# State space stage of a two-layer decoder: the closing normalisation of each batch on ScalarE instead of VectorE, and a new order of the passage to the second mixer

## The reference, cut to what matters

```python
x = _layernorm(x + _L1_attn_ref(x, L1_attn_W_in, ...), axis=-1)

def _layernorm(x, axis=-1, eps=1e-05):
    m = jnp.mean(x, axis=axis, keepdims=True)
    v = jnp.var(x, axis=axis, keepdims=True)
    return (x - m) / jnp.sqrt(v + eps)

# _L1_attn_ref(u, ...), 8 heads of 64, state 128
z, xBC, dt = jnp.split(u @ W_in, ...)
xBC = silu(conv of 4 taps over xBC)
x, B, C = jnp.split(xBC, ...)
y = ssd(x * dt, A * dt, B, C, chunk)  # per head: (C B^T * decay) (x dt)
y = (y + x * D) * silu(z)
var = jnp.mean(jnp.square(y), axis=-1, keepdims=True)
y = y * jax.lax.rsqrt(var + EPS) * norm_scale
return y @ W_out
```

## Time and profile before

| | us |
|---|---|
| runs before, median of 3 (lowest, highest) | 782.22 (782.18, 782.72) |
| the profiled execution's own time | 784.08 |
| its span in the trace | 782.3 |
| PE busy | 722.9 (92%) |
| DVE busy | 626.2 (80%) |
| POOL busy | 538.8 (69%) |
| ACT busy | 409.6 (52%) |

### The profile page before, as it was taken

How to read it: one execution, slowest core, us unless ns; L and a number is a source line. 1 busy time by engine, 2 the same in 40 slices (tenths; PEclk the granted TensorE clock), 3 DMA queues, 4 the chain that set the end, 5 groups by cost and what they waited for, 6 DMA issues and landing times. The chain is left out here.

```text
span 782.3 us, 13429 instructions
## 1 busy us (share of the span) xinstructions
PE 722.9 (92%) x4286; PEld 499.0 (64%) x4286; DVE 626.2 (80%) x1279; ACT 409.6 (52%) x656; POOL 538.8 (69%) x782
## 2 busy tenths in 40 slices
PE   6999999999997899999869999989899999999994
PEld 5777777654442577777547777765544447767783
DVE  3878877789798777774949999987899999887774
ACT  0656666610415444443667778880000338788885
POOL 2767888877773543331156777789877988999962
PEclk9999999999998799999979999999999999999998
DMA  8900000000400400000031112203000000000001
GB/s 282 372 11 2 2 2 2 2 1 0 162 0 24 182 1 2 1 1 1 24 114 43 62 60 67 69 1 124 0 1 1 0 2 0 9 15 14 21 20 37
DMA packets 12867, 33.89 MB, mean 43 GB/s; under 512 B 2688, under 2 KB 8064, under 8 KB 11520
## 3 DMA queue, kind: packets, MB, share of 16 engines
...
## 5 line engine op out<-in xcount | busy, mean ns | idle before, releaser
L1126 PE MATMUL bank<-XT,win_late 128*128 128x256 f32 x320 | 87.8, 402 | 4.4 <-DVE ss_xc L1376 4.2
L684 DVE TENSOR_REDUCE MIX<-m_pr 128x128 f32<-128x1024 f32 x64 | 77.4, 1210 | 0.7
L632 POOL TENSOR_TENSOR m_kv<-CTXT 128x512 f32<-128x512 f32 x64 | 65.0, 1039 | 10.4 <-PE bank L657 10.3
L632 POOL TENSOR_TENSOR m_kv<-XT,CTXT 128x512 f32<-128x512 f32 x64 | 67.7, 1081 | 5.8 <-PE bank L657 5.8
L1376 DVE SCALAR_TENSOR_TENSOR ss_xc<-bank,cw_late,ss_xc 128x254 f32<-128x254 f32 x144 | 66.5, 477 | 4.0 <-ACT ss_xc L1249 0.5
L1126 PEld LDWEIGHTS bank<-XT,win_late 128*128 128x128 f32 x320 | 56.9, 195 | 19.3 <-DVE ss_xc L1376 12.2
L655 PE MATMUL bank<-m_kv,toep 128*128 128x512 f32 x128 | 67.0, 605 | 0.2
L656 PE MATMUL bank<-m_kv,toep 128*128 128x512 f32 x128 | 66.2, 599 | 0.0
L657 PE MATMUL bank<-m_kv,toep 128*128 128x512 f32 x128 | 65.7, 595 | 0.0
L541 POOL TENSOR_TENSOR f_ve<-f_mv,eps 128x1 f32<-128x1 f32 x48 | 9.5, 199 | 80.4 <-DVE f_mv L946 61.1
L1703 PE MATMUL bank<-had_last,f_ht 128*128 128x256 f32 x256 | 60.6, 383 | 2.9 <-ACT f_ht L1786 1.6
...
## 6 DMA issues: line engine op xcount, KB each, us to landing
...
```

Of the source, the lines that this page charges most:

```text
L632: m = nc.gpsimd.tensor_tensor(KV[n % 3][:, c, :, :].rearrange("p (b j) i -> p b j i", b=HB), ki, vj, ALU.mult)
L684: nc.vector.tensor_reduce(head(MIX)[:, :, a, bass.ts(h, HB), :], PR[n % 2][:, :, :, :].rearrange("p c (b j) i -> p c b j i", b=HB), op=ALU ...
L1126: m = nc.tensor.matmul(bX[(NU * g + n) % 3][:, 0:GS_], win[:, h, off:off + P], XT[:, h, bass.ts(g, GS_)], start=(h == 0), stop=(h == C - 1))
```

## The change

`norm_x` moves from VectorE to ScalarE as an activation (scale rstd, bias nr). GpSimd's `rstd` gets a third, tiny instruction that makes nr = -mean * rstd. The sum y gets three tiles in place of two, so `residual(n)` waits for the norm of n - 3 and no longer for that of n - 2. In the steps, ScalarE does the norm of the odd batch 2(i-4)+1 behind the first `decay`, and that of the even batch 2(i-3) behind the second `gate`. The four `end` lists are written in a new order. The core of the diff:

```diff
-    Y, ST, MV, VE, RS = two("y", [P, D]), two("st", [P, 6]), two("mv", [P, 2]), two("ve", [P, 1]), two("rs", [P, 1])
+    Y = [ch.sb(f"ss_y{k}", [P, D]) for k in range(3)]
+    NR, ST, MV, VE, RS = two("nr", [P, 1]), two("st", [P, 6]), two("mv", [P, 2]), two("ve", [P, 1]), two("rs", [P, 1])
...
         def end(mix):
...
-            out_product(12); scan(15); x_turn(9, 12); mix(0); x_turn(10, 12); mix(1); mix(2); mix(3); mix(4); square_sum(12, 11); mix(5)
-            out_product(13); square_sum(13, 11); mix(6); mix(7); out_product(14); square_sum(14, 11); x_turn(11, 15); mix(8); out_product(15)
-            square_sum(15, 12); x_turn(12, 16); mix(9); x_turn(13, 16); mix(10); x_turn(14, 16); mix(11); x_turn(15, 16); mix(12); mix(13); mix(14)
+            out_product(12); mix(0); scan(15); x_turn(9, 12); mix(1); mix(2); mix(3); mix(4); square_sum(12, 10); mix(5); square_sum(13, 10)
+            x_turn(10, 14); mix(6); out_product(13); mix(7); out_product(14); square_sum(14, 11); x_turn(11, 15); mix(8); x_turn(12, 15)
+            out_product(15); square_sum(15, 13); x_turn(13, 16); mix(9); x_turn(14, 16); mix(10); x_turn(15, 16); mix(11); mix(12); mix(13); mix(14)
...
+        def norm_x(n):
+            if not 0 <= n < B:
+                return
+            act.wait_ge(s["offset"], n + 1)
+            nc.scalar.activation(X[:, n, :], Y[n % 3][:, :], ACT.Identity, scale=RS[n % 2][:, :], bias=NR[n % 2][:, :]).then_inc(s["normed"], 1)
...
             decay(GB * (i - 1))
+            norm_x(GB * (i - 4) + 1)
             tap3(i, 3)
...
             gate(i, 1)
+            norm_x(GB * (i - 3))
             silu(i)
...
-            upto(dve, s["normed"], n - 1)
-            nc.vector.scalar_tensor_tensor(Y[n % 2][:, :], bO[:, 0:D], RY[n % 2][:, :], X[:, n, :], ALU.mult, ALU.add).then_inc(s["out_free"], 1)
+            upto(dve, s["normed"], n - 2)
+            nc.vector.scalar_tensor_tensor(Y[n % 3][:, :], bO[:, 0:D], RY[n % 2][:, :], X[:, n, :], ALU.mult, ALU.add).then_inc(s["out_free"], 1)
...
             aggregate(GB * (i - 3) + 1)
-            norm_x(GB * (i - 3))
             matrix(GB * (i - 1) + 1)
...
             gated(GB * (i - 1))
-            norm_x(GB * (i - 3) + 1)
             aggregate(GB * (i - 2))
...
         def rstd(n):
             if not 0 <= n < B:
                 return
-            inv_std(pool, nc, T, MV[n % 2], VE[n % 2], RS[n % 2], T["eps5"], s["stats2"], s["eps_added"], s["rstd"], n)
+            upto(pool, s["normed"], n - 1)
+            k = n % 2
+            inv_std(pool, nc, T, MV[k], VE[k], RS[k], T["eps5"], s["stats2"], s["eps_added"], s["rstd"], n)
+            pool.wait_ge(s["rstd"], n + 1)
+            nc.gpsimd.tensor_scalar(NR[k][:, :], MV[k][:, 0:1], RS[k][:, :], -1.0, ALU.mult, ALU.mult).then_inc(s["offset"], 1)
...
         def end(mix):
-            args(14); args(15); rstd(10); x_dt(14); root(11); skip(14); x_dt(15); mix(0); skip(15); mix(1); mix(2); mix(3); mix(4); add_squares(12)
+            args(14); args(15); x_dt(14); root(11); skip(14); mix(0); x_dt(15); skip(15); mix(1); mix(2); mix(3); mix(4); add_squares(12); mix(5)
```

31 lines of the change are left out of this document (14 added, 17 removed).

## The result

The changed kernel took 788.08 us (median of 4 runs, 786.65 to 791.06) against 782.2 us of the kernel before on the same chip (4 runs, 780.57 to 782.72): a ratio of 1.0082, 95% interval 1.0061 to 1.0104. The forecast was 784.5 us with a range to 787.6. The sign was right, the size was not. Single executions that ran at a granted clock of 0.56 to 0.93 over their whole length (one each of `e_offring` and `e_nr_off`, two of the kernel before) are left out of every ratio, and of those two experiments' medians.

What follows compares the result with a forecast made beforehand. A gapless ring of ScalarE and GpSimd was taken to bound the steps. Three steps of +0.77 us (2.3), +0.1 and +0.3 made +2.7, the passage -0.4: +2.3 on the median 782.22 gave 784.5 us, range 780.0 to 787.6.

Steps and rivals of the forecast that it cites:

- The ring of ScalarE and GpSimd: Steps: ScalarE's gapless list, 11.23 us, then GpSimd's, 7.08 us, set the period of 18.31 us; VectorE's work is off it.
- the norm: Steps, ScalarE: the odd batch's norm stands between the two exponentials and adds 0.50 us to each step.
- the product: Steps, GpSimd: the product making nr, between `rstd` and `args`, adds 0.36 us to each step.
- The signs named for the steps: Steps 5 to 7: `floor` every 19.0 to 19.1 us, ScalarE gapless to odd `square`, VectorE idle about 3 us.
- The contention: Steps: GpSimd's second addition, slowed by VectorE's odd `matrix`, changes the step by -0.09 us, bounds 0 and -1.4.
- The early steps: Step 4 and the period before the three full ones: +0.1 us (between 0 and +0.4) and +0.3 us.
- The passage: Passage to mixer two, on TensorE's path: -0.4 us in all; bounds 0 to -1.5, or +3.4 with clock falls.
- 1.7 lost to the clock: Passage of before: behind the longer `variance` wait, clock 0.63 from 559.32 to 563.84 us cost 1.7 us; taken as regained.
- The clock behind the new waits: Rival, passage: TensorE's clock falls behind one or both 1.6 to 1.7 us waits, +1.7 each, 786.2 or 787.9; chance 0.22.
- The contention goes: Rival, steps: odd `matrix` done before the first addition, 1.4 us back against 0.86 added, about 780 us; chance 0.15.
- VectorE was the only bound: Rival, steps and passage: steps shorten by about 0.9 us each, passage's norms give 3 more, 775 us; chance 0.05.
- The passage gives more: Rival, passage: steps as forecast, passage gives 1 to 2.5 us, 782 to 783.5 us; chance 0.18.

Runs made afterwards that it cites:

- e_offring: Changed kernel with ScalarE's norm of the odd batch moved behind the squares of the odd batch: 784.12 us, ratio 1.0030 to the kernel before.
- e_nr_off: Changed kernel with GpSimd's product (nr) of the odd batch moved behind the next `args`: 783.87 us, ratio 1.0036 to the kernel before.
- e_nr_off_again: Changed kernel with GpSimd's product of the odd batch behind the next `args`, run once more for its trace: 782.97 us in one run.
- e_act_spend: Kernel before plus a needless 128x256 ScalarE activation between exponential and fourth tap in each step: 783.02 us, ratio 1.0023.
- e_all: Changed kernel, odd norm behind the squares, product behind next `args`, turns of batches 10 to 12 behind mixer steps 6 and 8: 778.95 us, ratio 0.9959 to before.
- second trace of after: Changed kernel, unaltered, measured and traced again beside the kernel before: 786.93 us, ratio 1.0062; span of the trace 785.1 us.
- e_best: Changed kernel, odd norm and product moved off the ring, passage lists in the order of before with ScalarE's norms: 780.22 us, ratio 0.9980 to before.
- second traces: Kernel before and changed kernel, both unaltered, each traced again: medians 782.77 and 786.93 us, spans 779.5 and 785.1 us.
- e_passage_again: Kernel before's steps (VectorE norms 0 to 9, no GpSimd product) with the changed passage, run again for a second trace: 784.5 us, one run.
- before, second trace: Kernel before, unaltered, run again for another trace: 782.77 us, ratio 1.0006 to itself; span of the trace 779.5 us.
- second measurement: Changed kernel, unaltered, run again beside the kernel before: 786.93 us (6 runs), ratio 1.0062 (1.0045 to 1.0080).
- the two parts: Changed steps with the passage lists in before's order, 784.52 us (1.0026); before's steps with the changed passage, 783.16 us (1.0012).
- e_norms_only: Kernel before with only the norms of batches 10 to 15 on ScalarE, three tiles of y, all orders kept: 779.78 us, ratio 0.9982.
- e_turns_later: Changed kernel, turns of batches 10 to 12 behind mixer steps 6 and 8, 13 to 15 a step later: 782.87 us, ratio 1.0009 to before.
- e_no_norm: Kernel before with VectorE's norms of batches 0 to 9 replaced by a tiny product: 780.87 us, ratio 0.9986.

## Why the prediction missed

**The bound of the steps: right.** The ring of ScalarE and GpSimd carries the period. `e_offring`, `e_nr_off_again` and `e_act_spend` give its terms one by one: 0.48 for the norm (forecast 0.50), 0.35 for the product (0.36). Both removed (`e_all`), the period falls from 18.95 to 18.12 us, by 0.83, the sum of the two. The signs named for the steps were there too. In the second trace of after no idle time stands on ScalarE from the `floor` of batch 8 to the odd `square`, and VectorE is idle for 3.04 us of that step, most of it ahead of the taps of units 1 and 3.

**What the relief of VectorE is worth.** The prediction had it at next to nothing. `e_all` and `e_best` have the norms off VectorE and nothing more on the ring. Their steps are shorter than before's: 18.12 instead of 18.31 us in the later periods, 17.84 instead of 18.78 from batch 6 to 8, and 1.7 us in all from batch 4 to 14. In the steps the move of the norms was worth that much; the two additions on the ring turned it into a loss.

**The contention: right in kind, too small.** The forecast was -0.09 a step. The period without falls is 18.95, +0.64 over before instead of +0.77, so with the two terms as measured (0.83) it was -0.19. GpSimd's second addition shows it in the second trace of after, 1.32 us where it was 1.53: the odd `matrix` starts 0.47 us behind the first addition, where it was 0.82.

```profile
476.63 0.75 POOL L1521 TENSOR_TENSOR ss_sq<-ss_sq 128x256 f32<-128x256 f32 x1 [1.22 <-ACT ss_sq L1291]
...
477.10 1.36 DVE L1400 TENSOR_TENSOR MIX<-MIX,ss_cbm 128x1024 f32<-128x1024 f32 x1
...
477.46 1.32 POOL L1523 TENSOR_TENSOR ss_sq<-ss_sq 128x128 f32<-128x128 f32 x1
```

**The early steps:** +0.3 and +0.1 forecast, +0.16 and -0.11 in the second traces (batch 4 to 6 and 6 to 8). **Sum at the passage:** +2.7 forecast; from the `floor` of batch 4 to that of batch 14 the second traces give 94.85 - 92.79 = +2.06 us. This term was 0.6 too large.

**The passage: here the prediction failed.** Forecast -0.4; with no fall behind a wait for `variance` on either side, and the one behind the scan on both, it is 69.15 us (`e_passage_again`, from the `floor` of batch 14 to mixer step 17) against 67.02 (before, second trace), **+2.1 us**. The 2.5 us of error are:

- 1.7 us: the step of the sum that put "1.7 lost to the clock" on the side of before, to be gained back. The fall was in the trace, but, to judge by the granted clock, not in three quarters of before's executions, and the median that the forecast was added to does not hold it. It could be seen beforehand: the profiled execution took 784.08 us and the median was 782.22. The text named this gap and then took the fall as part of what the median contains.
- 0.5 us: the two waits for `variance` were 1.82 and 1.96 us, not 1.7 and 1.6.
- The remaining 0.3 us are not traced to single rows.

With steps and passage put right the sum, with no fall behind a wait for `variance`, is 2.06 + 2.13 = +4.2 us, 786.4 us, and the measured difference is +4.7 (second measurement, 3.5 to 6.3 by its interval) or +5.9 (first). The medians of the two parts, +2.6 and +1.3 us, give +3.9; that of the passage alone has an interval of -0.2 to +2.1 us, so the passage's +2.1 rests on the traces.

The prediction's other figure, 784.08 + 2.3 = 786.4 us, lies near the result. In it the fall is in the time it starts from and is taken out again by the sum, so it cancels. That the rest fits as well is luck: the steps were 0.6 too large and the passage, but for the fall, 0.8 too small.

**The clock behind the new waits: the rival was real, and weighed wrongly.** The forecast took the wait of 1.76 us with no fall and that of 1.94 with one as a rule of length. There is no such rule in the 17 traces of this case (every run shown but the first of `e_nr_off`; waits before 395 us, those near 400 and 405 us, where the clock is low or just was, and one of 2.53 us in the first trace of after are left out):

| wait of TensorE | falls behind it |
|---|---|
| 1.43 us in feed-forward two | 0 of 17 |
| 1.31 to 1.59 us, copy of X in the steps | 0 of 9 |
| 1.59 to 1.93 us, a unit of TensorE near 412 us | 0 of 13 |
| 1.76 us at the end | 9 of 17 |
| 1.94 us, copy of X, step 5 of the changed steps | 0 of 6 |
| the same, step 6 | 6 of 6 |
| 1.94 to 1.97 us, `variance`, before's order | 3 of 4 |
| 1.81 us, `variance`, first of the changed order | 3 of 6 |
| 1.84 to 1.97 us, `variance`, second | 3 of 6 |
| 2.87 to 3.96 us, scan of batch 14 | 17 of 17 |

Behind a wait of 1.76 to 1.97 us a fall came in 24 of 49 cases, and where the wait stands matters more than its length: 0 of 6 in step 5, 6 of 6 in step 6. The honest price of one more such wait was its length plus about half of 1.6 us, with no wait counted as free. What decides the single case is open: the same wait at the same place differs from execution to execution at the end, and in the steps it is always the later of two equal ones. The price differs too: the same fall in step 6 cost 0.85 us in the first trace of after and 0.1 us in the second (from batch 10 to 14, 38.75 and 37.99 us against 2 x 18.95).

**Order and norms apart.** The passage of `e_norms_only`, 66.73 us from `floor` to step 17, is 0.3 us shorter than before's 67.02; with the changed lists on the same steps it is 69.15. So the new order costs 2.4 us and the norms give 0.3. The medians agree on the first: 1.0012 less 0.9982 is 2.3 us. The mechanism is in TensorE's list. In before, two steps of the mixer stand between `square_sum(13)` and the next turn of X; in after the turn of batch 10 stands right behind it and waits for VectorE to read the sum. With steps 6 and 8 ahead of the turns again (`e_turns_later`) the passage is 66.57 us.

**The rivals.** "The contention goes" (780 us) and "VectorE was the only bound" (775 us) did not happen, and `e_no_norm` says that the second could not: with all of VectorE's norms out of before's steps the kernel gains 0.14%, which its interval (0.9969 to 1.0003) does not tell from no change. "The passage gives more" had the sign wrong.
